# Cross-attention values: one product per half of the tokens instead of one per half of the heads

## What is computed

```python
def _mha(x, kv, Wq, Wk, Wv, mask, causal):
    m = mask[:, None]
    Q = jnp.einsum('bsd,hdk->bhsk', x, Wq) * m
    K = jnp.einsum('bsd,hdk->bhsk', kv, Wk) * m
    V = jnp.einsum('bsd,hdk->bhsk', kv, Wv) * m
    energy = jnp.einsum('bhsk,bhtk->bhst', Q, K)
    S = energy.shape[-1]
    lengths = jnp.sum(energy[:, :, 0, :] != 0, axis=-1)
    cols = jnp.arange(S)
    energy = jnp.where(cols[None, None, None, :] >= lengths[:, :, None, None], -jnp.inf, energy)
    ...
    score = jax.nn.softmax(energy / jnp.sqrt(jnp.asarray(dk, energy.dtype)), axis=-1)
    out = jnp.einsum('bhst,bhtk->bhsk', score, V) * m
...
z = _mha(x1, context, Wq2, Wk2, Wv2, mask1, causal=False)
x2 = _layernorm(x1 + z, ln2_g, ln2_b)
z = jnp.maximum(x2 @ fc1_w.T + fc1_b, 0.0) * mask0
z = (z @ fc2_w.T + fc2_b) * mask0
return _layernorm(x2 + z, ln3_g, ln3_b)
```

## Time and profile before

| | us |
|---|---|
| median of 3 runs (2827.41 to 2829.34) | 2828.35 |
| the profiled execution | 2827.12 |
| its span, first to last instruction | 2825.40 |
| mask phase and mlp phase | to about 1422 |
| causal phase | to about 1985 |
| cross phase | to the end |
| one turn of the cross phase | 51.0 |

### The profile page before, as it was taken

How to read it: one execution, slowest core, us unless ns; L and a number is a source line. 1 busy time by engine, 2 the same in 40 slices (tenths; PEclk the granted TensorE clock), 3 DMA queues, 4 the chain that set the end, 5 groups by cost and what they waited for, 6 DMA issues and landing times. The chain is left out here.

```text
span 2825.4 us, 68934 instructions
## 1 busy us (share of the span) xinstructions
PE 2768.9 (98%) x24736; PEld 2407.8 (85%) x24736; DVE 1759.9 (62%) x5436; ACT 1631.2 (58%) x4949; POOL 626.8 (22%) x755
## 2 busy tenths in 40 slices
PE   7999999999999999999999999999999999999997
PEld 6888888887888888888889999998888888888886
DVE  6666666667533332333377777777677777767766
ACT  6877777778211111111277777777766665656664
POOL 1110110111000000000013333333232433324333
PEclk9999999999999999999999999999999999999999
DMA  3111111113200000001021111113111111011100
GB/s 119 37 56 61 47 45 61 53 39 109 83 30 30 30 0 30 30 30 67 8 84 45 45 45 45 45 45 105 57 46 37 38 45 39 36 45 45 45 30 23
DMA packets 74820, 134.37 MB, mean 48 GB/s; under 512 B 10112, under 2 KB 10112, under 8 KB 74752
## 3 DMA queue, kind: packets, MB, share of 16 engines
q1 hardware_dynamic: 74752, 133.47, 13.5%
HBM read 99.90 MB, written 33.55 MB: 47 GB/s over the span
## 5 line engine op out<-in xcount | busy, mean ns | idle before, releaser
L2665 ACT ACTIVATE mlp_h<-mlp_f,mlp_b1col 128x512 f32<-128x512 f32 x128 | 88.3, 690 | 561.0 <-PE mlp_f L2833 561.0
L2833 PE MATMUL mlp_f<-mlp_xT_hi,mlp_w 128*128 128x512 f32 x1024 | 335.3, 389 | 0.0
L2748 DVE CAST mlp_hT_hi<-mlp_h 128x512 fp32r<-128x512 f32 x128 | 57.4, 448 | 432.8 <-ACT mlp_h L2665 432.7
L2851 PE MATMUL mlp_acc<-mlp_w,mlp_hT_hi 128*128 128x512 f32 x1024 | 316.7, 390 | 0.0
L725 ACT ACTIVATE mask_prob<-mask_scores,mask_low 128x256 f32<-128x256 f32 x512 | 236.9, 475 | 19.5 <-DVE mask_low L1229 19.1
L725 ACT ACTIVATE cross_prob<-cross_scores,cross_low 128x256 f32<-128x256 f32 x512 | 237.4, 499 | 6.9 <-DVE cross_low L1223 6.7
L1229 DVE CUSTOM_DVE_ANT_0 mask_scores<-mask_scores,mask_mask 128x256 f32<-128x256 f32 x512 | 201.0, 454 | 47.9 <-PE mask_scores L1822 47.8
L159 PE MATMUL causal_work<-causal_xT_hi,causal_w 128*128 128x256 f32 x1008 | 226.5, 296 | 0.0
L2833 PEld LDWEIGHTS mlp_f<-mlp_xT_hi,mlp_w 128*128 128x128 f32 x1024 | 192.2, 188 | 39.9
L2851 PEld LDWEIGHTS mlp_acc<-mlp_w,mlp_hT_hi 128*128 128x128 f32 x1024 | 191.2, 188 | 39.0
L725 ACT ACTIVATE causal_prob<-causal_scores,causal_low 128x128 f32<-128x128 f32 (+1 forms) x512 | 211.1, 434 | 18.3 <-DVE causal_low L1229 17.7
(11 more groups left out here) (333 smaller groups left out, 8269.1 us busy)
## 6 DMA issues: line engine op xcount, KB each, us to landing
cross_x_in<-after_attention SPq DMA_DIRECT2D x17, 512.0 KB, 3.7
mask_x_in<-in_x SPq DMA_DIRECT2D x16, 512.0 KB, 3.6
mask_c_in<-in_ctx SPq DMA_DIRECT2D x16, 512.0 KB, 4.4
mask_res<-in_x SPq DMA_DIRECT2D x16, 512.0 KB, 3.5
after_attention<-mask_res SPq DMA_DIRECT2D x16, 512.0 KB, 2.8
mlp_x<-after_attention SPq DMA_DIRECT2D x8, 1024.0 KB, 5.7
mlp_stage<-in_L_xattn_fc_w SPq DMA_DIRECT2D x8, 1024.0 KB, 5.1
after_layer<-mlp_y SPq DMA_DIRECT2D x8, 1024.0 KB, 4.3
```

Of the source, the lines that this page charges most:

```text
L2665: act.activation(h32[:, m % 2, :], F1[m % 2][:], ACT.Gelu, bias=b1col[:, m:m + 1]).then_inc(s["gelu"], 1)
L2748: dve.tensor_copy(hT[0][:, r, :], h32[:, r, :]).then_inc(s["h_hi"], 1)
L2833: ins = pe.matmul(F1[m % 2][:], W[2 * (m // 4)][:, a, k, m % 4 * P:(m % 4 + 1) * P], xT[p][:, k, :], start=(k == 0 and n == 0), stop=(k == ...
L2851: ins = pe.matmul(ACC[t][:], hT[a][:, m % 2, t * P:(t + 1) * P], W[2 * (m // 4) + 1][:, p, m % 4, :], start=(m == 0 and n == 0), stop=(m = ...
```

## The change

V is made by the tokens and no longer by the heads. `token_values(b, t)` is one product of 12 matmuls of 512 columns for all 16 heads of token half `t`, and fills a bank by itself. The first, `t = 0`, stands where (0, 0) and (0, 1) stood, six matmuls at each place. The second stands in one piece behind `turn_probs(b, 3)`, ahead of `queries(b, 3)` and of `attend(b, 0)`, and behind a wait for ACT's copy of the first. The places of (1, 0) and (1, 1) are empty. On ACT the second copy moves from behind `exps(b, 11)` to between `exps(b, 5)` and `exps(b, 6)`. `attend(b, 0)` now waits for both copies, `attend(b, 2)` for none. The mask phase and the causal phase keep `values`.

```diff
         def values(b, h):
             act.wait_ge(s["v_ps"], 2 * b + h + 1)
+            if cross:
+                if not isinstance(b, int) or b > 0:
+                    act.wait_ge(s["av_done"], KC * b)
+                act.activation(V[:, h, :, :], V_BANK[:].rearrange("p (h d) -> p h d", d=DH), ACT.Copy
+                               ).then_inc(s["v_ready"], 1)
+                return
...
                 copy(b, 3)
-                for u in (4, 5, 6):
-                    exps(b, u)
+                exps(b, 4)
+                exps(b, 5)
+                values(b, 1)
+                exps(b, 6)
...
                 exps(b, 11)
-                values(b, 1)
                 copy(b, 8)
...
+        def token_values(b, t, half=None):
+            ins = product(pe, V_BANK[:], lambda k, a: cT[a][:, k, t * P:(t + 1) * P], lambda k, c: W[2][:, c, k, :],
+                          half)
+            if half != 0:
+                ins.then_inc(s["v_ps"], 1)
...
             pe.wait_ge(s["copied"], UNITS * b + HC * (c + 1))
-            if c in (0, 2):
+            if cross and c == 0:
+                pe.wait_ge(s["v_ready"], 2 * b + 2)
+            elif not cross and c in (0, 2):
                 pe.wait_ge(s["v_ready"], 2 * b + 1 + c // 2)
...
-                values(b, 0, 0)
+                token_values(b, 0, 0)
                 turn_probs(b, 1)
...
-                values(b, 0, 1)
+                token_values(b, 0, 1)
...
                 turn_probs(b, 3)
+                pe.wait_ge(s["v_ready"], 2 * b + 1)
+                token_values(b, 1)
                 pe.wait_ge(s["qk_lo"], KC * b + 3)
                 queries(b, 3)
...
-                pe.wait_ge(s["v_ready"], 2 * b + 1)
-                values(b, 1, 0)
                 pe.wait_ge(s["len_ready"], KC * b + 3)
                 turn_probs(b, 6)
...
                 energies0(b, 3)
-                values(b, 1, 1)
```

More of the change, by code:

```diff
@@ L2526, in tensor @@
             pe.wait_ge(s["w_lo_done"], 3 * KC)
-            values(0, 0, 0)
+            token_values(0, 0, 0)
             turn_probs(0, 1)
```

## The result

The changed kernel takes **2881.51 us** (median of 4 runs, 2876.98 to 2886.63) against 2827.88 (2826.42 to 2829.34) for the kernel before on the same chip: a ratio of 1.019, interval 1.0171 to 1.0209. It is slower, as forecast, but by 53.6 us and not by 36. The profiled execution took 2883.4, its span 2881.7.

A forecast was written before the change was run, and what follows sets the result against it. TensorE's list of work was taken to bound each turn. Lost cover of 2.26 us in 14 turns plus 1.9 us for each of turns 0 and 15 gave 35.4 us, so 2864 us, range 2850 to 2882.

The forecast's parts named there:

- The two waits: TensorE would wait about 1.1 us ahead of `scores(b, 2)` and 1.74 us ahead of `feed1(b, 0)` each turn.
- The product itself: Two products of twelve 512-column matmuls replace four of 256 columns on TensorE: 5.50 us for 5.76, saving 0.26 a turn.
- The move to the front: `queries(b, 3)` and all behind come 2.62 us later; V about 0.7 us early; `qk(b, 3)` starts 2.26 us later.
- The first removed cover: Without `values(b, 1, 0)`, a new wait of about 1.1 us ahead of `scores(b, 2)`; the turn is 2.26 us late there.
- The second: Without `values(b, 1, 1)`, the wait ahead of `feed1(b, 0)` grows from 0.31 to 1.74 us; nothing is gained.
- The sum for the waits: 14 turns at 2.26 us, 31.6 us, with 1.9 us each for turns 0 and 15: together 35.4 us.
- First and last turns: Turns 0 and 15 lack part of the 2.26 us delay; 1.9 us was taken for each.
- the first rival: Clock also falls behind the new waits: up to 1.7 us a turn, 24 us in all (2888 us); chance 0.18.
- the nearest row: In the earlier trace, a 1.73 us wait at the end with no clock fall, taken as nearest to 1.74.
- The wide matmul is no quicker than `feed2`: Rival claimed the opposite: a 512-column product takes 1.44 us, giving about 2838 us; chance 0.02.
- V does not come late: Rival claimed ACT's copy comes over 0.7 us later than worked out, delaying `attend(b, 0)`: about 2874 us; chance 0.05.
- the second wait opened as the first did: Rival claimed only the wait ahead of `scores(b, 2)` opens, none ahead of `feed1`: about 2838 us; chance 0.05.

The follow-up runs named there:

- the second hole filled: Changed kernel with 14 dummy matmuls of 256 columns ahead of `feed1(b, 0)` alone: 2863.23 us, ratio 1.0129.
- both filled: Changed kernel with dummy matmuls in both waits, 8 ahead of `scores(b, 2)` and 14 ahead of `feed1(b, 0)`: 2864.16 us, ratio 1.0133.
- the high parts first on the changed kernel: Changed kernel with the high-part matmuls of `feed1(b, 0)` ahead of its low-part ones, its two banks exchanged: 2847.38 us, ratio 1.0069.
- the one with values by heads: Changed kernel with all four value products by heads, 256 columns wide, at the new places: 2886.26 us, ratio 1.0206.
- the first hole filled: Changed kernel with 8 dummy matmuls of 256 columns ahead of `scores(b, 2)` alone: 2882.92 us, ratio 1.02.
- the one with the keys moved: Changed kernel with `keys(b, 3)` behind `attended(b, 0)`, ahead of `scores(b, 2)`, and `qk(b, 3)` behind the turned tokens: 2858.36 us, ratio 1.0112.

## Why the prediction was right, and where it was not

The time lies in the range (2850 to 2882), 0.5 us below its upper end, and two of the four runs lie above that end: that the median is inside is luck. The two waits came as forecast and make 36 us; the other 18 are the falls of the clock, the rival to which I gave 0.18. By its steps:

- *The product itself* was right: 0.22 us a turn measured for the width, 0.26 in the sum. The chain has the second wide product together with `queries(b, 3)`, 24 matmuls; less the 1.43 of the queries that is 2.75 us, as forecast:

```profile
2321.19 4.18 PE cross_work L159 x24
```

- *The move to the front* was right in each step. ScalarE's timeline (start us, us, what, idle time) of this turn:

```profile
2323.97 0.60 ACT L717 ACTIVATE cross_v<-cross_work 128x512 f32<-128x512 f32 x1 [0.33 <-PE cross_work L159]
...
2328.10 0.60 ACT L707 ACTIVATE cross_qk_parts<-cross_work 128x512 fp32r<-128x512 f32 x1 [0.29 <-PE cross_work L159]
```

  V is there at 2324.57, 0.8 us ahead of `attend(b, 0)` at 2325.36; I had 0.7. `qk(b, 3)` starts at 2328.10, 0.11 behind the end of the keys (2326.36 + 1.63); I had allowed 0.07. VectorE takes over from there:

```profile
2328.74 0.69 DVE L1196 TENSOR_TENSOR cross_qk_parts<-cross_work,cross_qk_parts 128x512 fp32r<-128x512 f32 x1 [3.42 <-ACT cross_qk_parts L707]
...
2330.39 1.29 DVE L1188 TENSOR_TENSOR cross_xT_lo<-cross_scores,cross_xT_hi 128x512 fp32r<-128x512 f32 x2
```

  From `qk(b, 3)` to the scores it is 3.63 us, where I had 3.77 (half of the difference is that I took the start of the scores from the chain, 2308.76, and not from the timeline, 2308.69).
- *The first removed cover*: 0.98 us of wait, 1.1 forecast. *The second*: 1.74, as forecast. Together 2.26 us a turn, the forecast to the hundredth in the turns of 53.26 and 53.32. So close a fit is luck: `qk(b, 3)` came a little later than worked out and the way from it to the scores was a little shorter, and the two cancel. The sum for the waits, 35.4 us, is what the kernel with the second hole filled measured: 35.6.
- *First and last turns*: 1.9 us each in the sum. The last gave 1.74 with its hole filled, where no fall is in it; turn 0 about 3.3 in the changed kernel, where TensorE waits 3.19 us ahead of the scores for which it waited 1.52, and the clock is low for longer (granted 0.89 from 2000 to 2060, before 0.94):

```profile
2008.11 0.63 PE L1837 MATMUL cross_scores<-cross_qk_parts 32*128 32x256 f32 x12 [3.19 <-DVE cross_xT_lo L1188]
```

- **The step that failed is the choice in the first rival**: that the clock stays up behind the second wait. I went by the nearest row, the wait of 1.73 us at the end with no fall behind it, and gave the falls a chance of 0.18. Behind the same wait of 1.74 it fell in 12 of 15 cases here. The price that I gave for a fall, 1.7 us from the earlier trace rows, was close to the 1.55 measured, and with 12 falls at the measured price the sum is 2864 + 12 x 1.55 = 2882.6, 1.1 us from the result. One row where nothing happens had been held against one where something does, 0.2 us apart; they did not say which way 1.74 goes, and a case that a coin could settle got less than a fifth.
- Two of those rows say less than I read in them. Behind the wait of 1.52 us the row ends at 2008. Between 2010 and 2016 the clock of the kernel before did fall (columns as in the earlier trace rows), and what brought that about is not shown:

```profile
2010.00:2016.00 6.00, 5.29 (x41) 3.96 (x41) 3.26 (x9) 5.59 (x19) 0.00 (x0) 0.72 0.31 104
```

  And the wait of 1.94 us, the one with a fall behind it, came as 1.95 or 1.96 in three of the kernels above (the second hole filled, both filled, the high parts first on the changed kernel), with none. In the last of them, the row and the stretch around it (columns as in the earlier trace rows):

```profile
2031.47 0.62 PE L1819 MATMUL cross_probsT<-cross_qk_parts,cross_q 128*128 128x256 f32 x3 [1.96 <-POOL cross_q L519]
```

```profile
2028.00:2038.00 10.00, 8.04 (x90) 7.50 (x89) 5.69 (x15) 5.70 (x15) 1.44 (x4) 1.00 0.01 2
```

- That the waits cause the falls is shown: with the second one filled, shortened to 0.9 or 1.4 us, or taken out by the order within `feed1`, there was none in the turns, and with the first one filled they stayed. Why the same wait is followed by a fall in some turns and not in others is **open**: its length alone does not decide it, since it was 1.74 or 1.75 in all. Whether the moment at which it comes does, no run here tests.
- The other rivals fell. The wide matmul is no quicker than `feed2` (2.75 us for twelve of either), V does not come late, and the second wait opened as the first did.

## What to carry to other kernels

Work that an engine does while its next signal is under way costs nothing as long as it stands there. Moved to where nothing is awaited, it costs its full time there and leaves a hole behind, so before moving it, find for each place what signal comes due behind it and how early it is. Where a wait can't be avoided, start with the part of the next product whose operands are there, and look whether a few matmuls shorten the idleness enough to keep the clock up: here three useless ones were worth 17 us of 2881.

## What the runs showed of the hardware

- The granted clock behind one and the same idleness is not the same each time. Of 60 waits of 1.74 us (15 in each of the changed kernel, the one with values by heads, the one with the first hole filled and the one with the keys moved) 42 were followed by a fall from 2.4 to 1.2 GHz: 12, 11, 11 and 8. None of the waits of 0.9, 1.0 and 1.4 us in the turns was, and neither were single ones of 1.95 and 1.96 us in turn 0. The times of the changed kernel spread with its mean clock, too: its runs with a mean clock of 0.986 took 2883.4 and 2886.6, those with 0.989 and 0.991 took 2879.6 and 2877.0.
- A wait costs TensorE more than the idle time shown. The product behind it took 1.70 us where it takes 1.44 without: 0.26 more, and removing a shown wait of 0.31 us shortened the turn by 0.56.
- The idle times miss a wait within a product (2.20 us for twelve matmuls and not 1.43, 0.60 of it between matmuls); the durations in the chain show it.
